# A cross-attention stage in four groups under way at once, ahead of a gated local-attention loop on one core

## The chip, the core and the metric

The kernel runs on one core of a Trainium2 chip. The metric is the device time of one execution in microseconds. A profiled execution gives a span (first to last instruction) and a time of its own that is a little longer.

## What is computed

The input is x, 16 items of 128 tokens by 128 features in float32, and a context of the same shape.

```python
x = x + tanh(g_xattn) * xattn(layernorm(x), ctx)      # 1: the cross stage
x = x + tanh(g_ffn) * ffn(layernorm(x))               # 2: six layers

def xattn(query, value):
    q = query @ Wq.T + bq + qk_b
    v = value @ Wv.T + bv
    attn = softmax(q @ v.T / sqrt(128 / 16))
    return attn @ v
```

Each of the six layers of `ffn` is a local attention of 16 heads of 64 with rotary embeddings, normalised q and k, a window of 32 tokens and the one before it, and then a layer norm with a gated GELU product; both with a residual. Their weights are read once per layer.

## The kernel before

The program is written by hand for each engine: five instruction streams that meet on semaphores. It has two parts.

**The pair loop** takes 48 pairs of items (6 layers by 8 pairs), software-pipelined over three iterations by a `step` function per engine, with a fixed order on each. It is not changed. It reads x, normalised and transposed, from a tile R (features on the partitions), in a half that is shifted by one token. At its head TensorE waits until all of R is there (`h_ready`, 8 pairs) and until the eight weight blocks of layer 0 are split into an upper part (ScalarE, `upper_part`, L498) and a lower part (GpSimd, `lower_part`, L387). SyncE loads these blocks into a ring of four slots: block k + 4 is issued once the lower part of block k is done, and a load is issued only once the one before it has landed (L319 to L323). ScalarE's first instruction of the loop is L550 (xsh, the upper part of the first pair of R), then GpSimd makes xsl (L396), and TensorE's first products are L1049.

**The cross stage** comes ahead of it. It works on groups of 4 items, one 128x512 tile for each step. The loop `Fori(0, 2)` on each engine takes two groups (j = 0, 1) in a turn, each phase for both of them before the next phase:

- VectorE: statistics of the rows (L745, 4 per group), their aggregation (L751), after ScalarE's inverse deviation (L505, L507) four normalisations (L757) into xh4.
- TensorE: four turns (L993); for vT a 512-column product of Wv with the context (L997), for v four products (L999), for q a 512-column product (L1002); four products for the scores (L1006); four turns of p (L1012); four products for the output (L1017); four turns of the normalised result (L1022). A float32 product is two passes, a turn is one.
- ScalarE: copies out of PSUM (L515, L528), q and vT with their biases (L518, L519), exp with row sums (L523), the copies into R (L538).
- VectorE: v plus its bias (L774), row maxima and their negative (L778, L780), one over the sums times the gate (L784, L786), the gated residual into X1 (L791), then statistics and normalisation again, of X1.
- GpSimd: tables TC and TS (L468, L471), for each turn a copy of the context to a tile that TensorE reads (L480), and four lower parts. ScalarE's four upper parts of a turn stand behind its copies of p.

The second turn begins when the first has turned its results (`c_hT`, since xh4, X_ and the other tiles exist twice only). SyncE issues x and the context in halves (8 items each) and three arrays of constants; all engines wait for the first two halves and all constants together (`in_ready`, 5 transfers), and for the other halves at the second turn.

## Time and profile before

| | |
|---|---|
| median of 3 runs | 1537.67 us (1535.64 to 1537.88) |
| profiled execution, its own time | 1537.92 us |
| its span | 1536.0 us |
| mean granted TensorE clock | 0.971 |
| busy: TensorE (PE), its weight loads (PEld) | 94%, 76% |
| busy: VectorE (DVE), ScalarE (ACT), GpSimd (POOL) | 85%, 83%, 77% |

Times in rows are microseconds from the start of the span unless marked ns. A row of a timeline has the start, the time until the last of the merged instructions ended, the engine, the line, the operation, the tile written and those read, how many instructions are merged (x8), and in brackets the idle time before it and what ended that. SPq is SyncE's queue of DMA issues. Two instructions that follow one another on an engine overlap a little, so eight of them take less than eight times the duration of one. PEclk is the granted TensorE clock as a share of 2.4 GHz. A tile that shares its memory with another shows under the other's name: xh4, xhT4, qT4 and vT4 are "u", v4 is "sq", the x input is "OT", the context "v".

### The profile page before, as it was taken

The numbers are of one execution on the slowest core, as the hardware profiler recorded it, in microseconds if no ns is written. First come the engines' busy times: TensorE is split into PE (matmuls) and PEld (weight loads), VectorE is DVE, ScalarE is ACT, GpSimd is POOL, SyncE is SP. The second block draws the span as 40 slices with busy tenths as digits, with TensorE's granted clock in tenths as the row PEclk, the third lists the DMA queues.
The fourth block names the chain that finished last, engine by engine and source line by source line (L and its number), as shares of the span: only waits on it lengthen the run. The fifth ranks groups of instructions, "written<-read, shape, count | busy, mean of one in ns | idle before, by whom it ended". The sixth has DMA issues, their size and how long they took to land.

```text
span 1536.0 us, 84937 instructions
## 1 busy us (share of the span) xinstructions
PE 1439.3 (94%) x33248; PEld 1160.3 (76%) x33248; DVE 1301.4 (85%) x2401; ACT 1272.5 (83%) x2523; POOL 1184.8 (77%) x1166
## 2 busy tenths in 40 slices
PE   4579999999999999999999999999999999999986
PEld 3457777778778788777777777777877777887875
DVE  4577899899899899899989989988989978998962
ACT  3458889889889889889888988988988977888873
POOL 2287888888888888888888888888888866887850
PEclk9679999999999999999999999999999989999998
DMA  5111110111010011011012011012001001100101
GB/s 144 50 35 30 39 43 27 37 57 49 27 54 27 27 58 59 27 47 33 27 37 79 27 37 43 27 32 84 27 20 41 20 23 57 41 20 20 41 22 29
DMA packets 41464, 62.44 MB, mean 41 GB/s; under 512 B 3662, under 2 KB 30412, under 8 KB 41420
## 3 DMA queue, kind: packets, MB, share of 16 engines
q1 hardware_dynamic: 41420, 61.84, 13.6%
q8 instruction: 29, 0.48, 0.1%
q14 instruction: 15, 0.12, 0.0%
HBM read 18.84 MB, written 1.05 MB: 13 GB/s over the span
## 4 chain that ended last, share of the span: by engine, by line
PE 90%; issue 4%; DVE 1%; POOL 1%; ACT 0%; POOLq 0%; DVEq 0%; ACTq 0%
PE bank L1129 13%; PE bank L1049 13%; PE bank L1062 12%; PE bank L1141 11%; PE bank L1102 9%; PE bank L1050 9%; PE bank L1051 9%; PE bank L1176 4%; PE bank L1165 2%; PE bank L1167 2%; PE bank L1166 2%; PE bank L1149 2%; PE bank L1155 1%; DVE t L830 0%; POOL u L416 0%
## 5 line engine op out<-in xcount | busy, mean ns | idle before, releaser
L402 POOL TENSOR_TENSOR u<-u,t 128x512 f32<-128x512 f32 x384 | 490.6, 1283 | 30.3 <-DVE t L830 15.8
L416 POOL TENSOR_TENSOR u<-u,rn 128x512 f32<-128x512 f32 x384 | 390.7, 1044 | 41.9 <-ACT rn L568 41.9
L1049 PE MATMUL bank<-Wl,xsh 128*128 (+1 forms) x576 | 287.1, 498 | 22.6 <-issue 17.1
L422 POOL TENSOR_TENSOR P<-P,rs 128x512 f32<-128x512 f32 x192 | 196.4, 1043 | 132.1 <-DVE rs L858 132.1
L821 DVE TENSOR_TENSOR u<-bank,TC 128x512 f32<-128x512 f32 x384 | 259.8, 677 | 43.4 <-ACT sq L557 42.5
L557 ACT ACTIVATE sq<-bank 128x512 f32<-128x512 f32 x384 | 228.0, 606 | 71.7 <-PE bank L1051 70.1
L830 DVE TENSOR_TENSOR t<-bank,TS 128x512 f32<-128x512 f32 x384 | 257.8, 682 | 1.4
L814 DVE TENSOR_REDUCE ss<-sq 128x8 f32<-128x512 f32 x384 | 253.1, 669 | 6.5 <-issue 6.5
L1050 PE MATMUL bank<-Wh,xsl 128*128 (+1 forms) x576 | 231.2, 401 | 0.0
L1051 PE MATMUL bank<-Wh,xsh 128*128 (+1 forms) x576 | 230.5, 400 | 0.0
L582 ACT COPY qkT<-bank 128x512 f32<-128x512 f32 x384 | 209.9, 600 | 13.0 <-PE bank L1062 10.7
L1129 PEld LDWEIGHTS bank<-PT,vs 64*64 64x64 f32 x6144 | 175.3, 137 | 33.9 <-issue 33.7
L1129 PE MATMUL bank<-PT,vs 64*64 64x32 f32 x6144 | 192.7, 223 | 7.3 <-DVE t L830 2.0
L1129 PE MATMUL bank<-PT,v 64*64 64x32 f32 x6144 | 192.9, 222 | 4.0 <-issue 4.0
L838 DVE TENSOR_REDUCE nm<-bank 128x8 f32<-128x512 f32 x192 | 127.7, 686 | 78.9 <-PE bank L1102 78.9
L1141 PE MATMUL bank<-OT,WoS 128*128 128x256 f32 x768 | 181.6, 391 | 2.8 <-ACT OT L608 2.8
L1129 PEld LDWEIGHTS bank<-PT,v 64*64 64x64 f32 x6144 | 176.6, 138 | 3.6 <-issue 3.6
L1141 PEld LDWEIGHTS bank<-OT,WoS 128*128 128x128 f32 x768 | 145.5, 194 | 34.1 <-issue 15.4
L1049 PEld LDWEIGHTS bank<-Wl,xsh 128*128 128x128 f32 x576 | 110.1, 191 | 58.2 <-issue 35.5
L1062 PEld LDWEIGHTS bank<-shape_constants,u 64*128 64x128 f32 x3072 | 109.1, 141 | 59.3 <-issue 59.3
L1102 PE MATMUL bank<-qkT 64*32 64x64 f32 (+1 forms) x12288 | 150.1, 219 | 3.3 <-issue 3.3
L1102 PEld LDWEIGHTS bank<-qkT 64*32 64x32 f32 x12288 | 129.7, 106 | 29.7 <-issue 22.1
(98 smaller groups left out, 2764.3 us busy)
## 6 DMA issues: line engine op xcount, KB each, us to landing
vs<-v SPq DMA_DIRECT2D x96, 384.0 KB, 3.3
Wraw<-in_L_ffn_Wqkv_dram SPq DMA_DIRECT2D x72, 117.5 KB, 2.1
WoS<-in_L_ffn_Wo_dram SPq DMA_DIRECT2D x6, 512.0 KB, 3.8
W1h<-Wh SPq DMA_DIRECT2D x6, 341.0 KB, 2.5
W1l<-Wl SPq DMA_DIRECT2D x6, 341.0 KB, 2.9
Wraw<-in_L_ffn_W_dram SPq DMA_DIRECT2D x12, 116.0 KB, 2.2
OT<-in_x_dram SPq DMA_DIRECT2D x2, 512.0 KB, 5.7
v<-in_ctx_dram SPq DMA_DIRECT2D x2, 512.0 KB, 7.0
```

The costliest lines, as they stand in the source:

```text
L402: nc.gpsimd.tensor_tensor(u[:, r, c], u[:, r, c], t2[:, r, c % 2], ALU.add).then_inc(add_done[c], 1)
L416: nc.gpsimd.tensor_tensor(by_head(u[:, r, c]), by_head(u[:, r, c]), spread(rn[:, r, HC * c:HC * c + HC], HC, DH), ALU.mult).then_inc(qk_re ...
L814: nc.vector.tensor_reduce(ss[:, r, HC * c:HC * c + HC], by_head(square_out(c, r)), AX, ALU.add).then_inc(ss_done[c], 1)
L821: nc.vector.tensor_tensor(by_head(u[:, r, c]), by_head(bank_of("chunk", c, r)[:]), TC[:, layer(it - lag), c % 2].broadcast_to([128, HC, DH ...
L830: nc.vector.tensor_tensor(halves(t2[:, r, c % 2]), halves(bank_of("chunk", c, r)[:])[:, :, ::-1, :], TS[:, layer(it - lag), c % 2].broadca ...
L1049: nc.tensor.matmul(out, x[0], Wl[:, w], start=True, stop=False)
L1050: nc.tensor.matmul(out, x[1], Wh[:, w], start=False, stop=False)
L1051: nc.tensor.matmul(out, x[0], Wh[:, w], start=False, stop=True).then_inc(done, 1)
L1062: i = nc.tensor.transpose(bank_of(kind, k + g, r)[:, at:at + 64], src[p, 128 * t:128 * t + 128], ident[p, 64 * g:64 * g + 64])
L1102: i = nc.tensor.matmul(bank_of("scores", e, r)[64 * w2 + 32 * a:64 * w2 + 32 * a + 32, at + (32 if w == 0 else 0):at + 64], qkT[f, s, 0, t ...
L1129: i = nc.tensor.matmul(bank_of("values", h, r)[64 * e:64 * e + 64, 64 * t + 32 * w2:64 * t + 32 * w2 + 32], (vs, v)[w2][p, r, head:head + ...
L1141: i = nc.tensor.matmul(bank_of("Wo")[:, 0:2 * S], WoS[:, k], OT[:, k].rearrange("p r s -> p (r s)"), start=(k == 0), stop=(k == INNER // 1 ...
```

## The change

- The groups are four tiles each instead of two: all tiles of the stage, their small statistics tiles, and two PSUM banks per group (CROSS_A, CROSS_B) in place of two banks for each of four uses.
- The two-turn loops are gone. Each engine has one function for each step and group, and a written order of the calls, in which groups are at different steps.
- The inputs come in more parts, each with its semaphore: x and the context for group 0, for group 1, and for groups 2 and 3 together; the gate's two numbers alone; the other constants apart. An engine waits only for what a step reads.
- TensorE reads the context in place; GpSimd's copies of it are gone. GpSimd clears vs, which VectorE did.
- vT goes through ScalarE alone (its own semaphore), before v is computed, as both use bank B. p overwrites xh4, its turned form overwrites xhT4.
- ScalarE's upper parts 0 to 3 stand behind the copy of p of group 1, 4 to 7 one by one between later steps, each with a wait for its own block. GpSimd's lower parts come in one row behind the tables.

The diff, cut to its core (helpers that only wrap an instruction of before with its wait are left out):

```diff
-        cT = [t2[:, 0, g] for g in range(2)]
-        xh4, xhT4, qT4, vT4, p4, pT4, v4 = ([slots[g][j] for g in range(2)] for j in range(7))
+        xh4, xhT4 = ([u[:, k, g] for g in range(GROUPS)] for k in range(2))
+        qT4 = [t2[:, g // 2, g % 2] for g in range(GROUPS)]
+        vT4 = [qkT[:, g // 2, g % 2].rearrange("p t n -> p (t n)") for g in range(GROUPS)]
+        v4 = [PT[:, g // 2, g % 2] for g in range(GROUPS)]
+        p4, pT4 = xh4, xhT4
...
-        X_, V_, VT_, Q_ = K[0:2], K[2:4], K[4:6], K[6:8]
+        CROSS_A, CROSS_B = K[0:4], K[4:8]
...
+        def arrived(eng, sems_of_parts, g):
+            eng.wait_ge(sems_of_parts[min(g, 2)], 16)
...
         @block.sync
...
-            sp.dma_start(H[:, 0:PAIR], x[0:PAIR].rearrange("b s d -> s b d")).then_inc(in_ready, 16)
-            sp.dma_start(ctxS[:, 0:PAIR], ctxT[0:PAIR].rearrange("b d s -> d b s")).then_inc(in_ready, 16)
-            sp.dma_start(sc[:], shape_consts).then_inc(in_ready, 16)
-            sp.dma_start(fc[:], by_feature).then_inc(in_ready, 16)
-            sp.dma_start(ev[:], every_token.partition_broadcast(128)).then_inc(in_ready, 16)
-            sp.sem_inc(rest_ready, START)
-            sp.dma_start(H[:, PAIR:NB], x[PAIR:NB].rearrange("b s d -> s b d")).then_inc(rest_ready, 16)
-            sp.dma_start(ctxS[:, PAIR:NB], ctxT[PAIR:NB].rearrange("b d s -> d b s")).then_inc(rest_ready, 16)
+            items(x, H, "b s d -> s b d", 0, GB, x_in[0])
+            sp.dma_start(ev[:, 128:130], every_token[128:130].partition_broadcast(128)).then_inc(gate_in, 16)
+            sp.dma_start(fc[:], by_feature).then_inc(features_in, 16)
+            items(ctxT, ctxS, "b d s -> d b s", 0, GB, ctx_in[0])
+            sp.dma_start(sc[:], shape_consts).then_inc(shapes_in, 16)
+            items(x, H, "b s d -> s b d", GB, 2 * GB, x_in[1])
+            items(ctxT, ctxS, "b d s -> d b s", GB, 2 * GB, ctx_in[1])
+            sp.dma_start(ev[:, 0:128], every_token[0:128].partition_broadcast(128)).then_inc(rows_in, 16)
+            sp.dma_start(ev[:, 130:], every_token[130:].partition_broadcast(128)).then_inc(rows_in, 16)
+            items(x, H, "b s d -> s b d", 2 * GB, NB, x_in[2])
+            items(ctxT, ctxS, "b d s -> d b s", 2 * GB, NB, ctx_in[2])
...
         @block.gpsimd
...
-            pool.wait_ge(in_ready, 16 * N_INPUTS)
+            nc.gpsimd.memset(vs[0:32], 0.0).then_inc(consts_done, 1)
+            pool.wait_ge(rows_in, 32)
+            pool.wait_ge(shapes_in, 16)
...
-            with pool.Fori(0, NB // PAIR) as pair:
-                pool.wait_ge(rest_ready, pair * 32 + START)
-                for j in range(2):
-                    g = pair * 2 + j
-                    pool.wait_ge(c_v, g - 1 + START)
-                    pool.sem_inc(wait_met, 1)
-                    nc.gpsimd.tensor_copy(cT[j], ctxS[:, ds(g * GB, GB)].rearrange("p b d -> p (b d)")).then_inc(c_ctx, 1)
-                for i in range(4):
-                    lower_part(pair * 4 + i, pair * 4 + i)
+            for k in range(NB // 2):
+                lower_part(k, k)
...
         @block.scalar
...
+            def first_upper(k):
+                act.wait_ge(raw_loaded, 32 * (k + 1))
+                upper_part(k, k)
...
+            cross_rstd(0, 0)
+            cross_vT_out(0)
+            cross_rstd(1, 0)
+            cross_vT_out(1)
+            cross_rstd(2, 0)
+            cross_vT_out(2)
+            cross_x_out(0)
+            cross_rstd(3, 0)
+            cross_vT_out(3)
+            cross_q_out(0)
+            cross_x_out(1)
+            cross_q_out(1)
+            cross_exp(0)
+            cross_x_out(2)
+            cross_x_out(3)
+            cross_p_out(0)
+            cross_exp(1)
+            cross_q_out(2)
+            cross_q_out(3)
+            cross_p_out(1)
+            first_upper(0)
+            first_upper(1)
+            first_upper(2)
+            first_upper(3)
+            cross_exp(2)
+            cross_rstd(0, 1)
+            cross_exp(3)
+            cross_p_out(2)
+            cross_rstd(1, 1)
+            cross_p_out(3)
+            first_upper(4)
+            cross_h_out(0)
+            first_upper(5)
+            cross_h_out(1)
+            first_upper(6)
+            first_upper(7)
+            cross_rstd(2, 1)
+            cross_rstd(3, 1)
+            cross_h_out(2)
+            cross_h_out(3)
...
         @block.vector
...
+            cross_stats(0, 0)
+            cross_stats(1, 0)
+            cross_stats(2, 0)
+            cross_norm(0, 0)
+            cross_stats(3, 0)
+            cross_norm(1, 0)
+            cross_norm(2, 0)
+            cross_norm(3, 0)
+            cross_values(0)
+            cross_maxima(0)
+            cross_values(1)
+            cross_values(2)
+            cross_values(3)
+            cross_maxima(1)
+            cross_gates(0)
+            cross_attend(0)
+            cross_gates(1)
+            cross_stats(0, 1)
+            cross_maxima(2)
+            cross_attend(1)
+            cross_maxima(3)
+            cross_stats(1, 1)
+            cross_norm(0, 1)
+            cross_gates(2)
+            cross_gates(3)
+            cross_norm(1, 1)
+            cross_attend(2)
+            cross_attend(3)
+            cross_stats(2, 1)
+            cross_stats(3, 1)
+            cross_norm(2, 1)
+            cross_norm(3, 1)
...
         @block.tensor
...
+            def cross_v(g):
+                pe.wait_ge(c_vTs, g + 1)
+                for dst, src in zip(tiles(CROSS_B[g]), rows(ctxS, g)):
+                    i = nc.tensor.matmul(dst, src, wvT[:], start=True, stop=True)
+                i.then_inc(c_v, 1)
...
+            pe.wait_ge(features_in, 16)
+            pe.wait_ge(shapes_in, 16)
+            cross_vT(0)
+            cross_vT(1)
+            cross_v(0)
+            cross_vT(2)
+            cross_v(1)
+            cross_x(0)
+            cross_vT(3)
+            cross_q(0)
+            cross_x(1)
+            cross_v(2)
+            cross_scores(0)
+            cross_q(1)
+            cross_v(3)
+            cross_x(2)
+            cross_scores(1)
+            cross_x(3)
+            cross_p(0)
+            cross_q(2)
+            cross_o(0)
+            cross_q(3)
+            cross_p(1)
+            cross_scores(2)
+            cross_scores(3)
+            cross_o(1)
+            cross_p(2)
+            cross_p(3)
+            cross_h(0)
+            cross_o(2)
+            cross_o(3)
+            cross_h(1)
+            cross_h(2)
+            cross_h(3)
```

## Rows read from the trace of the kernel before

**Rows 1.** The page, part 4: the chain that ended last, shares by engine.
```profile
PE 90%; issue 4%; DVE 1%; POOL 1%; ACT 0%; POOLq 0%; DVEq 0%; ACTq 0%
```

**Rows 2.** Stretches: length, busy us (instructions) of each engine, granted clock, DMA share, GB/s.
```profile
9.80:40.11 30.31, 16.73 (x80) 12.70 (x80) 17.02 (x73) 14.77 (x41) 10.11 (x14) 0.85 0.39 107
40.11:68.15 28.04, 16.43 (x80) 12.08 (x80) 13.44 (x60) 13.81 (x40) 4.59 (x4) 0.74 0.11 29
68.15:119.40 51.25, 37.64 (x557) 28.16 (x559) 33.70 (x58) 26.11 (x53) 38.02 (x37) 0.70 0.15 45
119.40:1530.00 1410.60, 1367.37 (x32521) 1106.36 (x32517) 1233.53 (x2204) 1216.03 (x2388) 1131.58 (x1107) 0.99 0.13 38
```

**Rows 3.** Waits in the first 75 us: total, times, longest.
```profile
PE bank L993 <- DVE u L757: 18.3, 2, 14.3
```

**Rows 4.** Second halves' issues; landing times of x (first, last), then of the context.
```profile
3.82 0.38 SPq L308 DMA_DIRECT2D OT<-in_x_dram  x1
4.24 0.80 SPq L309 DMA_DIRECT2D v<-in_ctx_dram  x1
...
DMA to landing us min/median/max: 3.8/5.7/7.7
...
DMA to landing us min/median/max: 5.1/7.0/9.0
```

**Rows 5.** Timeline of VectorE in the cross stage.
```profile
9.26 0.16 DVE L738 TENSOR_TENSOR bqs<-feature_columns 128x1 f32<-128x1 f32 x1 [2.94 <-DMA every_token_rows<-in_every_token_dram]
...
12.38 2.94 DVE L757 TENSOR_SCALAR u<-OT,mv,rstd 128x128 f32 x8 [0.28 <-ACT rstd L507]
18.73 0.69 DVE L774 TENSOR_TENSOR sq<-bank,every_token_rows 128x512 f32<-128x512 f32 x1 [3.42 <-PE bank L999]
...
23.09 0.69 DVE L778 TENSOR_REDUCE mx<-bank 128x4 f32<-128x512 f32 x1 [1.06 <-PE bank L1006]
23.82 0.17 DVE L780 TENSOR_SCALAR nm<-mx 128x4 f32<-128x4 f32 x1
...
25.63 0.18 DVE L784 RECIPROCAL rc<-sum 128x4 f32<-128x4 f32 x1
25.84 0.23 DVE L786 TENSOR_SCALAR rg<-rc,tg 128x4 f32<-128x4 f32 x1
...
32.73 1.64 DVE L745 BATCH_NORM_STATS2 st<-X 128x6 f32 x8
34.30 0.62 DVE L751 BATCH_NORM_AGGREGATE mv<-st 128x2 f32<-128x6 f32 x8
35.26 2.14 DVE L757 TENSOR_SCALAR u<-X,mv,rstd 128x128 f32 x8 [0.34 <-ACT rstd L507]
...
58.44 2.16 DVE L791 SCALAR_TENSOR_TENSOR X<-bank,rg,OT 128x128 f32 x8 [1.41 <-PE bank L1017]
```

**Rows 6.** Timeline of TensorE's products and of one group's exp.
```profile
17.64 1.05 PE L999 MATMUL bank<-feature_columns,t 128*128 128x128 f32 x8
18.53 1.02 PE L1002 MATMUL bank<-u,feature_columns 128*128 128x512 f32 x2
...
24.02 0.37 ACT L523 ACTIVATE PT<-bank,nm 128x128 f32<-128x128 f32 x1 [0.56 <-DVE nm L780]
...
25.31 0.21 ACT L523 ACTIVATION_READ_ACCUMULATOR PT<-bank,nm 128x1 f32 x1
...
27.85 3.42 PE L1017 MATMUL bank<-sq,qkT 128*128 128x128 f32 x16
```

**Rows 7.** Timeline of ScalarE at the end of the cross stage.
```profile
65.76 2.37 ACT L538 COPY R<-bank 64x512 f32 x4 [2.10 <-PE bank L1022]
68.15 0.41 ACT L550 CAST xsh<-R 128x256 fp32r<-128x256 f32 x1
```

**Rows 8.** Timeline of the lower parts and of the block loads behind the first.
```profile
29.44 4.59 POOL L387 TENSOR_TENSOR Wl<-Wraw,Wh 128x470 f32 x4 [15.22 <-ACT Wh L498]
...
30.65 5.61 SPq L323 DMA_DIRECT2D Wraw<-in_L_ffn_Wqkv_dram  x5
```

More of the change, by code:

```diff
@@ L26 @@
 GB = 4
+GROUPS = NB // GB
 CROSS_HEADS = 16
@@ L290, in part_block, with rows, whole, by_item @@
             return W[:, ds((k // (NB // 2)) % 2 * W_SPLIT_SIZE + block * BLOCK, BLOCK)]
-        PAIR = 2 * GB
+        def rows(t, g):
+            return [t[:, GB * g + k] for k in range(GB)]
+        def whole(t, g):
+            return t[:, GB * g:GB * g + GB].rearrange("p b d -> p (b d)")
+        def by_item(ap):
+            return ap.rearrange("p (b d) -> p b d", b=GB)
+        def arrived(eng, sems_of_parts, g):
+            eng.wait_ge(sems_of_parts[min(g, 2)], 16)
         def tiles(t):
@@ L488, in _ @@
         def _(act):
[L489 removed]
+            for s in ACT_SEMS:
                 act.sem_inc(s, START)
[L491 removed]
+            act.wait_ge(gate_in, 16)
             nc.scalar.activation(tg[:], gate2[:], ACT.Tanh).then_inc(tanh_done, 1)
@@ new lines, in cross_p_out, with cross_h_out @@
+            def cross_p_out(g):
+                act.wait_ge(c_pT, g + 1)
+                nc.scalar.copy(pT4[g], CROSS_A[g][:]).then_inc(c_pTs, 1)
+            def cross_h_out(g):
+                act.wait_ge(c_hT, g + 1)
+                for k in range(2):
+                    p = slice(64 * k, 64 * k + 64)
+                    i = nc.scalar.copy(R[p, GB * g:GB * g + GB, k:k + S],
+                                       CROSS_A[g][p].rearrange("p (b s) -> p b s", b=GB))
+                i.then_inc(h_ready, GB // 2)
@@ L730, in _ @@
         def _(dve):
-            for s in DVE_SEMS + [c_st, c_mv, c_xh, c_vs, c_mx, c_nm, c_rc, c_rg, c_x1, c_hn]:
+            for s in DVE_SEMS:
                 dve.sem_inc(s, START)
@@ new lines, in cross_stats @@
+            def cross_stats(g, s):
+                if s == 0:
+                    arrived(dve, x_in, g)
+                else:
+                    dve.wait_ge(c_x1, g + 1)
+                for t, row in enumerate(rows((H, X1)[s], g)):
+                    i = nc.vector.bn_stats(st4[:, g, t], row)
+                i.then_inc(c_st[s], 1)
+                dve.wait_ge(c_st[s], g + 1)
+                for t in range(GB):
+                    i = nc.vector.bn_aggr(mv4[:, g, t], st4[:, g, t])
+                i.then_inc(c_mv[s], 1)
@@ new lines, in cross_attend @@
+            def cross_attend(g):
+                dve.wait_ge(c_rg, g + 1)
+                dve.wait_ge(c_o, g + 1)
+                for t, (dst, row) in enumerate(zip(rows(X1, g), rows(H, g))):
+                    i = nc.vector.scalar_tensor_tensor(out=dst, in0=tiles(CROSS_B[g])[t], scalar=rg4[:, g, t:t + 1],
+                                                       in1=row, op0=ALU.mult, op1=ALU.add)
+                i.then_inc(c_x1, 1)
+            cross_stats(0, 0)
+            cross_stats(1, 0)
@@ new lines, in cross_turn, with cross_x, cross_vT @@
+            def cross_turn(g, bank, src, done):
+                for dst, part in zip(tiles(bank), tiles(src)):
+                    i = nc.tensor.transpose(dst, part, ident[:])
+                i.then_inc(done, 1)
+            def cross_x(g):
+                pe.wait_ge(c_xh[0], g + 1)
+                cross_turn(g, CROSS_A[g], xh4[g], c_xT)
+            def cross_vT(g):
+                arrived(pe, ctx_in, g)
+                nc.tensor.matmul(CROSS_B[g][:], wvT[:], whole(ctxS, g), start=True, stop=True).then_inc(c_vT, 1)
```

236 lines of the change are left out of this document (86 added, 150 removed).

## The prediction

> **What bounds the kernel now.** I read the page first. The chain that ended last lies 90% on TensorE, over a span of 1536.0 us [rows 1]: the pair loop is TensorE's. The stretches then show that this is true only of the loop. From 119.40 us on TensorE is busy 1367.37 of 1410.60 us at a granted clock of 0.99. In the two turns of the cross stage, 30.31 and 28.04 us long, no engine is busy for much more than half: TensorE 16.73 and 16.43, VectorE 17.02 and 13.44, ScalarE 14.77 and 13.81 [rows 2]. That is a stage bound by latency: one phase at a time, two groups in it, everybody else waiting. The waits say the same: TensorE alone stood 18.3 us for the first normalised rows [rows 3]. The loop begins when ScalarE makes xsh, at 68.15 us, directly behind the last copies into R [rows 7]. So the question is one number: at what time L can that instruction start in the changed kernel? The loop's code is untouched, so the time changes by L minus 68.15, plus what a different start does to the loop's first iterations.
>
> **When the stage can start.** Before, all engines wait for five inputs; VectorE is released by the last of them at 9.26 [rows 5]. Afterwards group 0 needs 256 KB alone. The first half of x, 512 KB, landed 3.8 us behind its issue [rows 4], so I put the first quarter at 3.9 us; group 1, with 1.3 MB issued up to it, I put near 7.6, between the landings of the first and the last half. But VectorE's new order is stats 0, stats 1, stats 2, and only then norm 0, and group 2 comes with the last half of x. It was issued at 3.82 and landed 7.7 us later, at 11.5 [rows 4]. The bytes ahead of it are the same, split in more transfers, so I take 11.5 again; it stalls all of VectorE until then. The last ctx landed at 4.24 + 9.0 = 13.2 [rows 4], and TensorE's third product waits for it. The gain of the early start is thus small: norm 0 falls at 12.7 where it was at 12.38 [rows 5]. What the parts give is products of groups 0 and 1 done before.
>
> **VectorE's sum from there.** It is the busiest engine, so I add it up. One group costs: statistics half of 1.64 + 0.62, with the new wait of the aggregation for its own statistics 1.18 (the waits on its own result at 23.82 and 25.84 cost 0.03 to 0.04); four norms half of 2.14, 1.07; values 0.69; maximum and its negative 0.69 + 0.17; gates 0.18 + 0.23; four residuals half of 2.16, 1.08 [rows 5]. Left from 11.5: six statistics 7.1, eight norms 8.6, four values 2.8, four maxima 3.4, four gates 1.6, four residuals 4.3: 27.8 us. Unhindered it would end at 11.6 + 27.8 = 39.4.
>
> **Where it still waits.** TensorE at full clock takes 0.86 for a 512-column product (18.53 minus 17.64, the pitch, is 0.89 for eight 128-column ones) and 0.43 for four turns (four passes in place of eight) [rows 6]. From the last ctx: vT2 0.86, v1 0.89, x0 0.43, vT3 0.86, q0 0.86, x1 0.43, v2 0.89, scores 0 1.1, with 0.3 for a copy: 19.9. VectorE is free at 11.6 + 2 stats + 4 norms + values = 18.9: 1.0 of wait. Residual 0 wants exp (24.02 to the end of the row at 25.31, 1.5 [rows 6]), a turn 0.9, a copy 0.6, a product 1.05, two copies of x ahead on ScalarE 1.1 and handovers 0.3 behind the maximum's end at 20.8: 26.2, against 24.1 at which VectorE has done its other work: 2.1. Smaller ones 0.4. Together 3.5.
> **TensorE's clock.** Eight passes take 1.05 at the upper level; sixteen took 3.42 at 27.85, 0.21 each and so the lower level (1.2 GHz) [rows 6]. The stage now begins with products at 7 us; until some 13.7 I count them low, which costs 0.9 on the way to x0. Bounds: nothing, if it rises by 11; 2.0 if only at 17. TensorE has nothing to do between its last output product and norm 2, some 5 us in my layout, and behind that I count the lower level again.
> **VectorE beside GpSimd.** Eight norms took 2.94 while GpSimd built tables and copied, 2.14 alone [rows 5]. Norm 0 meets the tables; norms of the second half now meet the lower parts (eight of them, 4.59 per four [rows 8]), a meeting that the trace of before doesn't have: between 0 and 0.4 each for three of them by the nearest row, and up to a lower part's 1.15 by its length. I take 0.8 in all, nearer to the row; bounds 0.4 and 3.8.
> The Trainium skill (SBUF — State Buffer, Who interferes with whom) is against this change here: GpSimd and such a VectorE operation share a port pair, and the second "fully blocks" until the first is over. By it each of three norms could lose a whole GpSimd instruction; the sum would be 2.6 us longer, the time 1519.4 rather than 1516.8. The row of 2.94 is milder, though above the norm alone.
>
> **The tail and the sum.** Behind the last norm: handovers 0.1, a turn at the lower clock 1.15, two copies into R 1.19 (four took 2.37 [rows 7]): 2.4. L = 39.4 + 3.5 + 0.9 + 0.8 + 2.4 = 47.0.
> Is another engine later? In the two turns before ScalarE worked 28.6 us in all and TensorE 33.2, partly at the lower clock [rows 2]; spread over L, both fit. GpSimd's four ctx copies go (nothing gained, they were covered), and the memset of vs moves to it, before 4 us, where it is idle. The weights: upper part 0 is now behind p_out 1, near 29; then lower part 1.15, four block loads at 2.2 (five issues in 5.61 [rows 8]), upper and lower part 1.8: the eighth lower part at 42 or so, 5 us ahead of L. If that cover went, every us beyond would be paid. SP's loads 8 to 11 and the copies to W1h follow, done by 49; up wants them only two iterations later.
> Gain: 68.15 − 47.0 = 21.1. I count the loop's start as before: its first 51 us ran at a mean clock of 0.70 [rows 2], and how that pattern falls now is unknown, 3 us either way. Profiled execution: 1537.92 − 21.1 = 1516.8; its own time is 0.25 above the median of the runs shown, which I leave.
>
> **Rivals.**
> *The clock stays low in the stage (9%).* The first turn had 0.85 and the second 0.74 with TensorE busy at about 55% [rows 2]. All of it low, TensorE's products and turns left from 13.2 (20 us at the upper level: 0.86, 0.89 and 0.43 each, for four groups less the three done) take 40 and 8 more of gaps and tail: L near 62, a time of 1532. Low for half the stage, L near 53, 1523. Against it: TensorE's work is now denser. For it: pauses of 1.9, 1.5 and 5 us in my layout. The skill's rule (TensorE: Matmul & The Clock Gate, Part 1: The HAM clock gate) that the throttled state is the default and activity releases it would give this rival where my gaps count as idleness; the trace agrees that it fell behind thin stretches.
> *The stage gains, the loop gives back (7%).* VectorE, ScalarE and GpSimd start the loop in other relations, with more of it at the lower clock: 5 to 8 us back, 1522 to 1525.
> *Better than the sum (10%).* Clock high from 11 on and into the loop, no collision with GpSimd: L 44.5 and 2 us less in the first iterations, 1512.
> *Weights become the bound (2%).* If a block load took 4 us rather than 2.2, the eighth lower part comes at 49 and L is overtaken by 2 us: 1519.
> *Slower than before (2%).* One mechanism: the loop's low clock. In the loop a us at the lower level costs half a us where TensorE bounds. The first 51.25 us had some 31 at that level, as (1 − 0.70) / 0.5 of them [rows 2]. It decides once over 42 us more are low (twice 21.1); with 60 more the time is 1516.8 + 30 = 1547. The kernel's behaviour from 119.40 on (0.99) speaks against it.
> That the change doesn't do what it says (1%): an engine's order could make the groups run one behind another; at 28 us for two groups as now nothing is gained but the 5 us of the input wait, 1533. The written orders speak against it.
>
> **Numbers.** The forecast has 69%, 1516.8. The range 1511 to 1524 takes L from 44.5 to 51 and the loop's 3 us; the lowest of the better case and the half-low clock fit in, the rest is left out. 0.2% is 3.1 us, about what a measurement of this kernel can tell from no change. Only the last mechanism ends slower, 0.02; a hundredth lies within, and the rest, 0.97, is faster by more.
>
> **What would show it.** The first statistics at about 4 us, norm 0 near 12.7, VectorE nearly without a break from 20 on, TensorE's last turns behind norms 2 and 3, xsh at 47, the eighth lower part before 43, and the loop from its second layer on moved by a constant. Norm 0 much before 12, xsh behind a lower part, or a stretch of clock 0.5 in the middle of the stage would show steps wrong. A loop that is longer than 1467.85 us from xsh to the end would point to the second rival.

## The result and the profile after

The changed kernel takes 1519.82 us (median of 4, 1516.7 to 1520.05), the kernel before in the same comparison 1536.66 (1535.21 to 1537.88): a ratio of 0.9878, 95% interval 0.9859 to 0.9897. Forecast were 1516.8 us and a range of 1511 to 1524. The profiled execution took 1519.64 us, 18.3 less than that of before (1537.92).

The page of the changed kernel: its span, the granted clock in 40 slices and the chain's shares (as in [rows 1]):

```profile
span 1517.7 us, 84772 instructions
...
PEclk9789999999999999999999999999999999999998
...
PE 91%; issue 4%; DVE 1%; POOL 1%; ACT 0%; POOLq 0%; DVEq 0%; ACTq 0%
```

Its stretches, columns as in [rows 2]; the first is the cross stage, the second the loop, the others are inside and behind the stage's last third:

```profile
0.00:48.93 48.93, 29.26 (x160) 21.73 (x160) 31.11 (x136) 29.99 (x83) 15.18 (x19) 0.91 0.48 132
48.93:1517.60 1468.67, 1403.76 (x33088) 1132.19 (x33088) 1269.39 (x2264) 1242.40 (x2440) 1170.26 (x1144) 0.98 0.13 38
36.40:39.70 3.30, 3.30 (x18) 3.30 (x17) 2.19 (x9) 2.21 (x5) 2.24 (x2) 0.50 0.26 73
39.90:43.10 3.20, 0.41 (x4) 0.17 (x2) 3.05 (x17) 2.63 (x6) 0.90 (x2) 1.00 0.34 91
43.30:53.30 10.00, 5.07 (x15) 3.82 (x16) 3.64 (x12) 4.30 (x9) 2.15 (x3) 0.50 0.47 150
```

The stage now ends at 48.93 us where it ended at 68.15. Its work is what it was: VectorE is busy for 31.11 us of the 48.93, where the two turns before had 17.02 and 13.44 of 58.35 [rows 2]. The low stretches are now short ones: 36.4 to 39.7 lies on the output products of the last two groups, 39.9 to 43.1 is TensorE's pause at 1.00, and 43.3 to 53.3 takes in the last turns and the loop's first products. The 0.91 leaves the head out: the view has 1.00 there, but TensorE's first four passes, from 8.25 on, took 3.93 us, 0.98 each, where a pass of the same product took 0.43 at the upper level (two of them between 17.32 and 18.18). In the page the clock is 9 from the fourth of the 40 slices to the last but one, and the chain is TensorE's to 91%. The loop takes 1517.7 − 48.93 = 1468.8 us against 1467.85: 0.9 us more, which is less than it scatters between executions (below).

ScalarE's timeline at the end of the stage, to be held against [rows 7]:

```profile
46.54 2.37 ACT L547 COPY R<-bank 64x512 f32<-64x512 f32 x4 [2.50 <-PE bank L1069]
48.93 0.41 ACT L606 CAST xsh<-R 128x256 fp32r<-128x256 f32 x1
```

VectorE's timeline in the stage, to be held against [rows 5] (from 13.54 on its waits, in brackets, come to 3.8 us in all):

```profile
13.54 0.87 DVE L801 BATCH_NORM_STATS2 st<-OT 128x6 f32<-128x128 f32 x4 [3.39 <-DMA OT<-in_x_dram]
...
14.74 1.53 DVE L812 TENSOR_SCALAR u<-OT,mv,rstd 128x128 f32<-128x128 f32 x4
...
17.38 3.13 DVE L812 TENSOR_SCALAR u<-OT,mv,rstd 128x128 f32<-128x128 f32 x12
...
21.54 0.69 DVE L824 TENSOR_REDUCE mx<-bank 128x4 f32<-128x512 f32 x1 [0.43 <-PE bank L1094]
...
24.63 0.69 DVE L824 TENSOR_REDUCE mx<-bank 128x4 f32<-128x512 f32 x1 [0.39 <-PE bank L1094]
...
27.46 1.13 DVE L839 SCALAR_TENSOR_TENSOR X<-bank,rg,OT 128x128 f32<-128x128 f32 x4 [1.60 <-PE bank L1105]
...
38.28 1.13 DVE L839 SCALAR_TENSOR_TENSOR X<-bank,rg,OT 128x128 f32<-128x128 f32 x4 [0.82 <-PE bank L1105]
39.98 1.12 DVE L839 SCALAR_TENSOR_TENSOR X<-bank,rg,OT 128x128 f32<-128x128 f32 x4 [0.58 <-PE bank L1105]
...
43.39 2.97 DVE L812 TENSOR_SCALAR u<-X,mv,rstd 128x128 f32<-128x128 f32 x8
```

SyncE's issues of the last half of x and of the context (against [rows 4]):

```profile
5.41 0.43 SPq L317 DMA_DIRECT2D OT<-in_x_dram  x1
5.89 2.68 SPq L317 DMA_DIRECT2D v<-in_ctx_dram  x1
```

The landing times of the parts of x, over all of them:

```profile
DMA to landing us min/median/max: 2.8/5.6/8.1
```

Those of the context:

```profile
DMA to landing us min/median/max: 4.2/6.3/9.1
```

The last half of x lands at 5.41 + 8.1 = 13.5 and the context at 5.89 + 9.1 = 15.0. Before it was 11.5 and 13.2.

TensorE's timeline at the end of the stage: sixteen passes of the output products of groups 2 and 3 in 3.58 us, then a pause until the last two groups are normalised:

```profile
36.30 3.58 PE L1105 MATMUL bank<-PT,u 128*128 128x128 f32 x16
...
45.38 2.14 PE L1069 MATMUL bank<-shape_constants,u 128*128 128x128 f32 x8 [5.07 <-DVE u L812]
```

GpSimd's timeline at the same time: two lower parts, the second of them beside the last eight norms, and then nothing until xsl:

```profile
42.31 2.42 POOL L407 TENSOR_TENSOR Wl<-Wraw,Wh 128x470 fp32r<-128x470 f32 x2 [2.30 <-ACT Wh L512]
49.50 0.72 POOL L416 TENSOR_TENSOR xsl<-R,xsh 128x256 fp32r<-128x256 f32 x1 [4.77 <-issue]
```

The second of these lower parts by itself, and the eight norms one by one (the shortest, the median and the longest in ns, then the starts of the first and the last):

```profile
43.44 1.29 POOL L407 TENSOR_TENSOR Wl<-Wraw,Wh 128x470 fp32r<-128x470 f32 x1
...
L812 DVE TENSOR_SCALAR u<-X,mv,rstd x8: 316/334/1202, 43.4 to 46.0; 128x128 f32<-128x128 f32 x8
```

Seven of the eight norms took about 0.33 us. One, from 43.62 to 44.82, took 1.20: it ended 0.1 us behind the lower part, at 44.73. The earlier lower part ended as the norms began.

### The profile page after: what moved, and what is told of

It is laid out like the page before. It is cut to its first block, busy times and chain, and to the rows that moved or that the text cites. A ratio compares the mean times of both kernels' runs of the same rounds, so it can differ in the third digit from the quotient of the medians.

```text
span 1517.7 us, 84772 instructions
## 1 busy us (share of the span) xinstructions
PE 1433.0 (94%) x33248; PEld 1153.9 (76%) x33248; DVE 1300.5 (86%) x2400; ACT 1272.4 (84%) x2523; POOL 1185.4 (78%) x1163
## 4 chain that ended last, share of the span: by engine, by line
PE 91%; issue 4%; DVE 1%; POOL 1%; ACT 0%; POOLq 0%; DVEq 0%; ACTq 0%
PE bank L1252 13%; PE bank L1172 13%; PE bank L1185 12%; PE bank L1264 12%; PE bank L1225 9%; PE bank L1173 9%; PE bank L1174 9%; PE bank L1299 4%; PE bank L1288 3%; PE bank L1290 2%; PE bank L1289 2%; PE bank L1272 2%; PE bank L1278 1%; POOL u L422 0%; POOL u L436 0%
## 5 line engine op out<-in xcount | busy, mean ns | idle before, releaser
L1172 PE MATMUL bank<-Wl,xsh 128*128 (+1 forms) x576 | 286.4, 497 | 23.7 <-issue 17.4
L900 DVE TENSOR_TENSOR u<-bank,TC 128x512 f32<-128x512 f32 x384 | 259.8, 677 | 41.8 <-ACT sq L613 40.8
L1264 PEld LDWEIGHTS bank<-OT,WoS 128*128 128x128 f32 x768 | 144.8, 194 | 34.0 <-issue 15.5
L1225 PE MATMUL bank<-qkT 64*32 64x64 f32 (+1 forms) x12288 | 150.4, 219 | 5.2 <-issue 5.2
```

What stands on the lines that cost most here:

```text
L900: nc.vector.tensor_tensor(by_head(u[:, r, c]), by_head(bank_of("chunk", c, r)[:]), TC[:, layer(it - lag), c % 2].broadcast_to([128, HC, DH ...
L1172: nc.tensor.matmul(out, x[0], Wl[:, w], start=True, stop=False)
L1225: i = nc.tensor.matmul(bank_of("scores", e, r)[64 * w2 + 32 * a:64 * w2 + 32 * a + 32, at + (32 if w == 0 else 0):at + 64], qkT[f, s, 0, t ...
L1264: i = nc.tensor.matmul(bank_of("Wo")[:, 0:2 * S], WoS[:, k], OT[:, k].rearrange("p r s -> p (r s)"), start=(k == 0), stop=(k == INNER // 1 ...
```

## The experiments

All of them are measured by the start of xsh in their profiled execution, since the loop behind it, unedited, scatters by more than most edits are worth. Where rounds were timed, the median stands too. xsh scatters as well: two executions of one kernel (e8 and f1) are 1.8 us apart, and the statistics of group 2, which start when the last half of x lands, began at 13.54 and 12.61 in two executions of the changed kernel. The profiles of e1 to e4, of e5 to e8, and of the f runs with the repetition also come from three chips. A difference of xsh under 2 us between two of them shows nothing by itself; the durations and waits in the rows do.

**e1: the overlap undone.** All tiles, banks, semaphores, transfers stay; only the three written orders change.

```diff
             cross_stats(0, 0)
             cross_stats(1, 0)
+            cross_norm(0, 0)
+            cross_norm(1, 0)
...
+            cross_norm(0, 1)
+            cross_norm(1, 1)
             cross_stats(2, 0)
-            cross_norm(0, 0)
...
```

> Same tiles, banks, inputs in parts and no copies of the context, but the written orders take groups 0 and 1 through all steps and then groups 2 and 3. Theory (the gain is the overlap of four groups): xsh, the loop's first instruction on ScalarE, goes from 48.9 back to about 61 us (58 to 64), span near 1530. Rival (the gain comes from the early inputs, the missing copies and the missing turn boundary): xsh at 50 to 53, span near 1520.

xsh came at 64.62, span 1531.0. Its VectorE timeline, norms 0 and 1, statistics and norms of the second pair, and the last norms:

```profile
9.94 3.13 DVE L812 TENSOR_SCALAR u<-OT,mv,rstd 128x128 f32<-128x128 f32 x8
...
35.13 0.86 DVE L801 BATCH_NORM_STATS2 st<-OT 128x6 f32<-128x128 f32 x4
...
59.94 2.11 DVE L812 TENSOR_SCALAR u<-X,mv,rstd 128x128 f32<-128x128 f32 x8
```

And xsh in its ScalarE timeline:

```profile
64.62 0.40 ACT L606 CAST xsh<-R 128x256 fp32r<-128x256 f32 x1
```

The first pair of groups takes 25.2 us from its norms to the next pair's statistics, and the second 23.7 from its norms (38.36) to the end of its last ones. Of the 19.2 us that the change gained in the stage, 15.7 (64.62 − 48.93) are the overlap of the four groups, and 3.5 the rest. Some 2 us of the 15.7 are TensorE's lower level in e1's second pair: its eight turns took 2.14 and its four passes for vT 2.70, where they take 1.04 and 1.72 (four times 0.43) at the upper level. Of the 3.5, the first norms' earlier start is 2.4 (9.94 against 12.38); what the rest is made of wasn't told apart. The expected 61 was too low by 3.6, outside its 58 to 64; the rival's 50 to 53 is out.

**e2: the seven input transfers of before, with their gating.** The eleven issues that they replace are left out.

```diff
+            sp.dma_start(H[:, 0:2 * GB], x[0:2 * GB].rearrange("b s d -> s b d")).then_inc(x_in[0], 16)
+            sp.dma_start(ctxS[:, 0:2 * GB], ctxT[0:2 * GB].rearrange("b d s -> d b s")).then_inc(x_in[0], 16)
+            sp.dma_start(sc[:], shape_consts).then_inc(x_in[0], 16)
+            sp.dma_start(fc[:], by_feature).then_inc(x_in[0], 16)
+            sp.dma_start(ev[:], every_token.partition_broadcast(128)).then_inc(x_in[0], 16)
+            sp.dma_start(H[:, 2 * GB:NB], x[2 * GB:NB].rearrange("b s d -> s b d")).then_inc(x_in[2], 16)
+            sp.dma_start(ctxS[:, 2 * GB:NB], ctxT[2 * GB:NB].rearrange("b d s -> d b s")).then_inc(ctx_in[2], 16)
...
+                eng.wait_ge(x_in[0], 80)
```

> The changed kernel with the seven input transfers of before and their gating (all engines wait for the first five, groups 2 and 3 for the last two). Theory (VectorE's chain starts at the landing of the last half of x, which the parts made later, 13.5 where it was 11.5): xsh at 47.5 us (46.5 to 49), no loss. Rival (the early start of groups 0 and 1 is worth what it looks like, 3 to 4 us): xsh at 52 or later.

xsh at 48.54, span 1518.0. The statistics of group 2 and norm 0 in its VectorE timeline:

```profile
11.96 0.84 DVE L799 BATCH_NORM_STATS2 st<-OT 128x6 f32<-128x128 f32 x4
...
13.13 1.09 DVE L810 TENSOR_SCALAR u<-OT,mv,rstd 128x128 f32<-128x128 f32 x4
```

They begin 1.6 us earlier than with the parts (11.96 and 13.54), though nothing starts before 9.5. The parts gave the four-group stage nothing that these runs can see: they let groups 0 and 1 run ahead and made the last half late. Of the 1.6, 1.34 are there at the first maximum (20.20 against 21.54), and 0.4 at xsh. Most of the loss lies at the output products of group 2, for which VectorE waited 1.48 us rather than 0.82: this execution had a lower clock from 33.1 to 39.9, twice as long as the changed kernel's 36.3 to 39.8. Another 0.2 is the last eight norms, 3.16 us.

**e3: the rotary rows last.**

```diff
-            sp.dma_start(ev[:, 130:], every_token[130:].partition_broadcast(128)).then_inc(rows_in, 16)
             items(x, H, "b s d -> s b d", 2 * GB, NB, x_in[2])
             items(ctxT, ctxS, "b d s -> d b s", 2 * GB, NB, ctx_in[2])
+            sp.dma_start(ev[:, 130:], every_token[130:].partition_broadcast(128)).then_inc(tabs_in, 16)
```

> The 384 KB broadcast of the rotary rows is issued behind all x and context, so that the last half of x lands some 1.3 to 1.8 us earlier. Theory (VectorE's chain from that landing): norm 0 at 13.2 rather than 14.7; xsh 47.6, or 48.3 if GpSimd's tables, now at 15 to 19 us, slow norms 1 to 3 as they slowed norm 0. Rival (TensorE and ScalarE's chain is late anyway): xsh at 48.9.

xsh at 47.25, span 1516.1. Its VectorE timeline, statistics of group 2, norm 0 and norms 1 to 3:

```profile
11.44 0.87 DVE L801 BATCH_NORM_STATS2 st<-OT 128x6 f32<-128x128 f32 x4 [1.64 <-DMA OT<-in_x_dram]
...
12.64 1.08 DVE L812 TENSOR_SCALAR u<-OT,mv,rstd 128x128 f32<-128x128 f32 x4
...
14.83 4.75 DVE L812 TENSOR_SCALAR u<-OT,mv,rstd 128x128 f32<-128x128 f32 x12
```

The last half of x is there 2.1 us earlier and norm 0 stands at 12.64. GpSimd's tables now run beside norms 1 to 3: twelve normalisations in 4.75 us, where the changed kernel took 3.13. The end came 1.7 us earlier all the same, earlier than both of the theory's times. Against the changed kernel's second execution (below) it is 1.2 at the landing and 1.5 at the end. The last context came earlier too: TensorE, which had waited 1.77 us for it, went on at 13.10 without a wait. So the end of the stage follows the last inputs, even with the dearer norms; e3 doesn't tell x from the context.

Later in the same execution the four norms of group 1 met a lower part, and it shows on one of them alone:

```profile
35.47 1.18 POOL L407 TENSOR_TENSOR Wl<-Wraw,Wh 128x470 fp32r<-128x470 f32 x1 [2.47 <-ACT Wh L512]
...
L812 DVE TENSOR_SCALAR u<-X,mv,rstd x4: 340/341/1280, 34.7 to 35.5; 128x128 f32<-128x128 f32 x4
```

**e4: the last lower parts behind the norms.**

```diff
             for k in range(NB // 2):
+                if k == NB // 2 - 2:
+                    pool.wait_ge(c_xh[1], GROUPS)
                 lower_part(k, k)
```

> GpSimd's last two lower parts wait until the last normalisations are done. Theory (the eight norms at 43.4 took 2.97 us where eight alone take 2.14, because a lower part runs beside them): 2.14 again, xsh at 48.1 us, the lower parts at 45.6 to 48. Rival (something else slows them): 2.97 and xsh at 48.9. If the lower parts become the last thing the loop waits for, TensorE's first product comes over 1.5 us behind xsh.

The last eight norms in its VectorE timeline:

```profile
44.51 2.14 DVE L814 TENSOR_SCALAR u<-X,mv,rstd 128x128 f32<-128x128 f32 x8
```

2.14 us for eight, as alone, none over 0.345, so the lower part beside them was the cause of the 2.97. But xsh came at 49.22, not 48.1. Its x had landed 0.4 later (statistics of group 2 at 13.92), and the lower clock lay at 34.7 to 41.5, all over the output products of groups 2 and 3; the statistics behind them began 0.7 us later against those of group 2's x than before (28.17 and 27.48). The gain and the loss were of one size.

**e5: norm 0 and norm 1 ahead of the statistics of group 2.**

```diff
             cross_stats(0, 0)
+            cross_norm(0, 0)
             cross_stats(1, 0)
+            cross_norm(1, 0)
             cross_stats(2, 0)
-            cross_norm(0, 0)
             cross_stats(3, 0)
-            cross_norm(1, 0)
```

> Only VectorE's order is changed: norm 0 and norm 1 stand directly behind their statistics, before those of group 2, so that they don't wait for the last half of x. Theory (norm 0's wait is covered, since TensorE's turns of group 0 stand in its own order behind the product that waits for the last context, 15.0 us): norm 0 at about 7.5 us and norm 1 at 10.5, but the first maximum still at 21.5 and xsh at 48.9 within 0.5. Rival (VectorE's sum from the landing of x is the path, as the prediction's sum has it): two norms less in it, xsh at 46.8.

xsh at 51.09, later than theory and rival had it. Norm 0, the statistics of group 2 and the first maximum in its VectorE timeline:

```profile
7.10 1.12 DVE L812 TENSOR_SCALAR u<-OT,mv,rstd 128x128 f32<-128x128 f32 x4 [0.69 <-ACT rstd L518]
...
13.38 0.87 DVE L801 BATCH_NORM_STATS2 st<-OT 128x6 f32<-128x128 f32 x4 [0.44 <-DMA OT<-in_x_dram]
...
23.03 0.69 DVE L824 TENSOR_REDUCE mx<-bank 128x4 f32<-128x512 f32 x1 [1.26 <-PE bank L1094]
```

Norm 0 was ready 7.6 us earlier and the first maximum stood 1.5 us later. The granted clock was 0.50 from 14.9 to 18.3, where the changed kernel's first execution had the upper level. Was that the edit's doing? The repetition answers it.

**The changed kernel once more, unedited.**

> The changed kernel once more, unedited, for the scatter of one execution against another. Theory (where TensorE's lower level falls differs between executions; in the first execution it stood at 36.3 to 39.8, in e5 and e7, whose edits come later, also at 15 to 19): xsh between 48.5 and 50.5, the loop between 1464 and 1470, both moved by where the lower level falls. Rival (the level's place is a property of the program): xsh 48.9 and a loop of 1468.8 again, both within 0.3.

The median was 1518.79 (1516.78 to 1522.16; ratio 0.9905, 0.9875 to 0.9935). Its profile has xsh at 48.72, the loop at 1466.2, and a low stretch of its own from 14.0 to 17.4. The statistics of group 2 and the first maximum in its VectorE timeline:

```profile
12.61 0.87 DVE L801 BATCH_NORM_STATS2 st<-OT 128x6 f32<-128x128 f32 x4 [3.28 <-DMA OT<-in_x_dram]
...
22.28 0.69 DVE L824 TENSOR_REDUCE mx<-bank 128x4 f32<-128x512 f32 x1 [1.26 <-PE bank L1094]
```

The low stretch, columns as in [rows 2]:

```profile
14.00:17.40 3.40, 3.14 (x9) 2.11 (x10) 3.37 (x17) 1.12 (x3) 0.54 (x2) 0.50 0.30 77
```

So such a stretch comes without the edit too; it belongs to the execution. From the statistics of group 2 to the first maximum it is 22.28 − 12.61 = 9.67 us here and 23.03 − 13.38 = 9.65 in e5. With like clocks, the place of norms 0 and 1 is worth nothing, as e5's theory had it: TensorE's turns of group 0 stand behind the product with the last context. Both these executions had VectorE wait 1.26 us for TensorE ahead of the maximum. At the upper level VectorE waited there too, 0.43 us, so TensorE was the later one in all three. In the first execution, with the clock high, it was 21.54 − 13.54 = 8.00. The low stretch there costs 1.7 us (9.67 − 8.00), of which 0.16 is a context that came later behind x (1.65 us rather than 1.49). The theory of this run held; its rival's loop of 1468.8 within 0.3 is out.

**e7: TensorE kept busy in its pauses.** The extra turns go to a free bank and are read by nobody.

```diff
+            def keep_busy(n):
+                for k in range(n):
+                    nc.tensor.transpose(tiles(CROSS_A[0])[k % 4], ident[:], ident[:])
...
+            pe.wait_ge(c_pTs, 1)
+            keep_busy(12)
             cross_p(2)
+            pe.wait_ge(c_pTs, 1)
+            keep_busy(12)
             cross_p(3)
...
+            pe.wait_ge(h_ready, START + GB // 2)
+            keep_busy(36)
             cross_h(2)
```

> The changed kernel with 12, 12 and 36 extra turns of the identity into a bank that is free then, in TensorE's pauses before p 2, p 3 and h 2; nobody reads them. Theory (the lower clock at 36.3 to 39.8 and from 43.2 on, behind pauses, makes the output products of groups 2 and 3 take 3.6 us rather than 2.0 and the last turns 2.1 rather than 1.3): no lower level before the loop, output products 2.0, xsh at 47.2 to 47.8, and the loop's first 5 us at the upper level too. Rival (the clock is of no weight, VectorE hides it): xsh 48.9; or the extra turns stand in the way: over 49.5.

Its TensorE timeline:

```profile
37.85 1.95 PE L1105 MATMUL bank<-PT,u 128*128 128x128 f32 x16
...
40.50 4.09 PE L1114 MATMUL bank<-shape_constants 128*128 128x128 f32 x36
46.21 0.66 PE L1069 MATMUL bank<-shape_constants,u 128*128 128x128 f32 x4 [1.62 <-DVE u L812]
...
50.73 0.77 PE L1182 MATMUL bank<-Wl,xsh 128*128 128x512 f32 x1 [2.83 <-POOL xsl L416]
```

The output products took 1.95 us rather than 3.58, the last turns ran at the upper level (0.66 for four), and from the first maximum to xsh it was 49.29 − 23.09 = 26.2 us against 27.4 in the changed kernel. xsh itself came at 49.29, because this execution too had the low stretch at 15.5 to 18.9, ahead of all extra turns. The repetition, with no extra turns and no low stretch there, took 48.72 − 22.28 = 26.4 for the same way: the net gain behind the first maximum is about 1 us. The waits for the output products, 0.82 and 0.58 in the changed kernel, are gone in both, which is 1.4; other delays hide a part of it, 0.67 for the deviations in the repetition and, here, 0.93 for a lower part beside the norms of group 1. The loop's first products were low again from 49.6 on. Of the expectation, the products' 2.0 held; xsh at 47.2 to 47.8 and a loop start at the upper level did not.

**e8: tables last and GpSimd out of the way.** e3 and e4 together, and the tables wait for norm 3.

```diff
             pool.wait_ge(tabs_in, 16)
+            pool.wait_ge(c_xh[0], GROUPS)
...
+                if k == NB // 2 - 2:
+                    pool.wait_ge(c_xh[1], GROUPS)
```

> Tables last as in e3, and GpSimd stays off VectorE's normalisations: it makes the tables only behind norm 3, and the last two lower parts behind the last norm. Theory (the two meetings cost 4.75 - 3.1 = 1.6 and 2.97 - 2.14 = 0.8): norms at 1.05 to 1.1 each, xsh 46.0 (45.5 to 46.8), apart from what TensorE's clock does. Rival (the first norms are covered as in e5's theory, only the last ones count): 46.8 to 47.3.

xsh at 45.53, span 1509.7. The norms in its VectorE timeline:

```profile
12.51 1.08 DVE L815 TENSOR_SCALAR u<-OT,mv,rstd 128x128 f32<-128x128 f32 x4
...
14.70 3.13 DVE L815 TENSOR_SCALAR u<-OT,mv,rstd 128x128 f32<-128x128 f32 x12
...
41.02 2.11 DVE L815 TENSOR_SCALAR u<-X,mv,rstd 128x128 f32<-128x128 f32 x8
```

1.08 for four, 3.13 for twelve, 2.11 for eight. It is 3.4 us better than the changed kernel in the stage, and at the edge of the theory's bounds. 2.2 us of it are x, which landed at 11.31 rather than 13.54. That xsh doesn't stand by itself: the same kernel once more (f1) came to 47.37.

**e6 and f2: new orders.** On top of e8 norms 0 to 2 stand directly behind their statistics and TensorE turns group 0 before the products of groups 2 and 3; e6 has ScalarE's upper parts 4 and 5 behind a copy into R, f2 ahead of it.

```diff
             cross_p_out(3)
+            first_upper(4)
             cross_h_out(0)
+            first_upper(5)
             cross_rstd(2, 1)
-            first_upper(4)
-            first_upper(5)
             cross_h_out(1)
```

> e8 with new written orders on VectorE, ScalarE and TensorE: each norm directly behind its statistics, group 0 turned before the products of groups 2 and 3, first upper parts spread over ScalarE's early gaps. Theory (VectorE's sum from 11.5 less the two early norms, 25.7, with 2.5 of waits, 0.5 for the clock and 2.4 of tail, is 42.6 at best and the handovers leave about 44.5): xsh at 44.5 (43.5 to 46), span near 1513. Rival (some other chain, TensorE's or ScalarE's, is as long as VectorE's): xsh 46 or later.

> e6 with ScalarE's upper parts 4 and 5 ahead of the copies into R, so that lower parts 4 and 5 are over before the last norms. Theory (e6 missed 44.5 because its last eight norms took 2.96 beside lower parts 4 and 5): the norms 2.14, xsh 45.0 to 45.4. Rival (ScalarE's two more casts delay the copies and the last deviations): xsh 46 or later.

e6 has xsh at 46.11 and a span of 1505.3; f2 45.91 and 1509.6, a median of 1512.17 (1510.94 to 1518.21, ratio 0.9865, 0.984 to 0.989). The last eight norms in e6's VectorE timeline:

```profile
40.58 2.96 DVE L815 TENSOR_SCALAR u<-X,mv,rstd 128x128 f32<-128x128 f32 x8
```

And in f2's, with the four of group 1 ahead of them:

```profile
35.34 2.09 DVE L815 TENSOR_SCALAR u<-X,mv,rstd 128x128 f32<-128x128 f32 x4
...
41.23 2.11 DVE L815 TENSOR_SCALAR u<-X,mv,rstd 128x128 f32<-128x128 f32 x8
```

f2's theory is right about the last norms, but the end moved by 0.2 us only. The meeting had moved rather than gone: of the four norms of group 1, 1.11 us in e6, one took 1.33 beside a lower part of 1.23. In e6 the new orders got the first maximum 1.3 us earlier than e8's (18.25 and 19.52), but the second came at 23.54 behind a wait of 1.74 for TensorE, where e8 had it at 22.61 with none. The sum of VectorE's work no longer sets the length by itself, and e6's theory, 44.5, missed; its rival, 46 or later, holds. f2's median is f1's within 0.2 us, so the new orders gained nothing that the rounds can see.

**f1 and f3: e8 timed, and e8 with TensorE kept busy up to the loop** (12, 12 and 30 extra turns as in e7, and 18 behind the last group's turns).

> e8 once more, timed in rounds. Theory: xsh 45.5 to 46.5, 3 to 4 us ahead of the changed kernel in the stage, ratio to before near 0.9845 (1512 to 1514). Rival (e8's total was luck with the clock in the loop): xsh the same, the median at 1516 or more.

> e8 with extra turns of the identity in TensorE's pauses: 12 before p 2 and p 3, 30 before h 2, 18 behind h 3, up to the loop's first product. Theory (e7 showed no lower level from 20 us to the loop, and 1.2 us less from the first maximum to xsh, but the level fell in the pause behind h 3): no lower level from about 20 us on into the loop, xsh 44.8 to 45.3, the loop's first 5 us at 2.4 GHz, and 2 to 3 us off the total of f1. Rival (the level falls in the loop anyway, some iterations later): xsh the same, the total within 1 us of f1's.

f1: median 1512.34 (1511.78 to 1513.17), ratio 0.9855 (0.9831 to 0.9879), xsh at 47.37. f3: 1512.27 (1511.5 to 1514.53), 0.9857 (0.9833 to 0.9882), xsh at 47.22. In the same rounds the changed kernel stood at 1518.79 and the kernel before at 1534.94. So the rotary rows last and GpSimd out of the way are worth some 6 us of the total, of which the stage's profiles show 1.4 to 3.4; the extra turns add nothing. f1's theory held in the total (1512 to 1514) and not in xsh (45.5 to 46.5). Its xsh was 1.8 us behind that of e8, the same kernel: x landed 0.8 later, and the lower clock lasted from 32.7 to 39.6 where e8 had it from 32.6 to 36.0. f3 had the loop's first 5 us at the upper level, but the lower one from 43.3 to 46.7, xsh 2 us later than expected, and a total within 1 us of f1's, as its rival had it. f3 shows what comes next when VectorE is early, in ScalarE's timeline:

```profile
41.45 0.58 ACT L515 CAST Wh<-Wraw 128x470 fp32r<-128x470 f32 x1 [2.81 <-DMA Wraw<-in_L_ffn_W_dram]
```

Upper part 7 waited 2.81 us for its block of weights, and the inverse deviations of groups 2 and 3 stand behind it in ScalarE's order, so the last norms waited 2.39 us for them. The repetition of the changed kernel had the same on a smaller scale, in its ScalarE timeline:

```profile
42.33 0.58 ACT L512 CAST Wh<-Wraw 128x470 fp32r<-128x470 f32 x1 [1.10 <-DMA Wraw<-in_L_ffn_W_dram]
```

## Why the prediction was right, and by how much its steps were off

The direction, the mechanism and the range held; the forecast was 3.0 us below the median. Of the 2.8 by which it missed the profiled execution, 1.9 are xsh and 0.9 the loop. By its own steps:

- *When the stage can start*: the step that failed. It took the last half of x at 11.5 and of the context at 13.2, since the bytes ahead were the same. They came at 13.5 and 15.0: SyncE, with more transfers ahead, issued the last x at 5.41, not at 3.82, and it took 8.1 us to land, not 7.7. In the repetition it landed at 12.6, so 0.9 of the 2.0 is scatter of this one execution. xsh was missed by 1.9 us (48.93 against 47.0); the landing alone is 2.0. Of the two inputs it is the context that the first maximum hung on: VectorE waited 0.43 us for TensorE there, and TensorE's row from the last context to the end of scores 0 took 6.5 us (15.03 to 21.51), where the prediction added up 6.7. The other terms cancelled, which is luck: waits and clock 3.8 against 4.4, GpSimd 1.3 against 0.8, the tail 2.6 against 2.4. In the six executions with the changed kernel's orders (both of its own, e2, e3, e4, e7) the statistics of group 2 began between 11.44 and 13.92 and xsh came 35.3 to 36.6 us behind them.
- *Norm 0 is hardly earlier*: right in kind, 14.74 against 12.38 before. It is even later. The first statistics came at 5.78, not at about 4: the sum of two biases ahead of them waits for the feature columns (5.70). Nothing hung on it, as x of group 2 was the stop.
- *VectorE's sum, 27.8, with waits 3.5, clock 0.9, GpSimd 0.8*: 33.0 from the last half of x to the last norm's end; measured 46.36 − 13.54 = 32.8 (the last norm ends at 43.39 + 2.97). The waits were 0.43, 0.39, 1.60, 0.82 and 0.58, 3.8 in all, where waits and clock together were put at 4.4. GpSimd's part was under-sized: norm 0 took 1.53 (0.46 more) and the last eight 2.97 (0.83 more), 1.3.
- *TensorE's clock*: put at 0.9 on the way to x0. The first products did run at the lower level, but cost nothing, as the next one waited 1.77 for the last context; in the repetition the level fell again during that wait and cost 1.5 to 1.7. The sign that the prediction named, a stretch of 0.5 inside the stage, came at 36.3 to 39.8, and the 1.4 of waits for output products hang on it (none in e7 and in the repetition). The prediction had only the pause behind them low.
- *VectorE beside GpSimd*: the price of a meeting was misjudged. "The row of 2.94 is milder" doesn't hold: in the kernel before, the slow ones of those eight norms took 0.55, 0.63 and 0.63 us beside GpSimd instructions of 0.54, 0.61 and 0.61. The Trainium skill (SBUF — State Buffer, Who interferes with whom) says that the second of the two "fully blocks", and the traces agree: one norm of 1.20 us beside a lower part of 1.29 in the changed kernel, one of 1.28 beside 1.18 in e3, the rest of those eight and four at 0.32 to 0.34. e4 and e8 take GpSimd away and the norms go back to 2.14 and 2.11. What was fewer than the rule's three is the meetings: one of norm with lower part, and two short ones of norm 0 with the tables. That its 1519.4 is so near the 1519.64 is luck, the landing's doing.
- *The tail*: 2.4 predicted, 48.93 − 46.36 = 2.57.
- *The weights as cover*: the eighth lower part was over at 44.7, not 42 (the terms given add up to 40.8), and 4 us ahead of xsh. It was late because upper parts 6 and 7 stand behind the copy into R of group 1, which waited for TensorE until 40.35. That sum looked only at the loop's wait. It missed that ScalarE's wait for block 7 stands ahead of the last inverse deviations: 1.10 us of it in the repetition, 2.81 in f3.
- *The loop as before, 3 us either way*: 1468.8 against 1467.85, and in the repetition 1466.2.
- *Rivals*: the low clock in the stage didn't decide (0.87 on the mean from 13.54 to xsh, up from 0.85 and 0.74 before). The groups did overlap, as e1 shows by undoing it. The loop gave nothing back beyond its scatter.

What stays open is the loop. Its length from xsh to the end was 1468.8 and 1466.2 in the changed kernel, 1466.4, 1469.5, 1468.9, 1467.4 and 1465.7 in e1 to e5, 1464.6 in e7, 1463.9, 1464.2, 1463.7 and 1463.2 in f1, e8, f2 and f3, and 1459.2 in e6, with the same instructions throughout. The granted clock's low stretches fall differently in each. Its middle is the same: from the sixth pair's xsh to the 41st's it is 1022.7 and 1022.8 us in the changed kernel's two executions, 1022.7 in e8 and 1022.8 in f1. The differences lie at its two ends. The first five pairs took 153.6, 150.0, 150.4 and 145.2 us, so one kernel (e8 and f1) scatters there by 5 us. Still, the five profiles with GpSimd out of the way have the five shortest loops of all, and f1's five timed executions all lie 3.5 us or more below the changed kernel's eight (1511.78 to 1513.17, 1516.7 to 1522.16). That is hard to put down to chance, but no run shows what makes the loop shorter. Of the 6 us by which f1 beats the changed kernel in rounds, it is the larger part if f1's own profile is the measure (1.4 in the stage), and half if e8's is (3.4).

## What to carry to other kernels

In this stage no engine was busy for more than 59% [rows 2], and more independent items at different steps paid. Its new length could be had in advance by adding up the busiest engine from the landing of the last input that its written order waits for, plus its waits for the others, here above all for TensorE behind the last context. Here that was right within 0.2 us, with luck among the terms; the same kind of sum missed e6 by 1.6, where VectorE waited 1.84 and 1.74 for TensorE ahead of the first two maxima and one of its last norms met a lower part. Splitting inputs so that the first groups can start early is worth little if an engine's order meets the last input soon after (e2), and each further transfer delays that one by its issue, 0.43 to 0.55 us here. Once a stage is packed, check what stands behind every wait on an in-order engine: here a cast that waited for weights held up two small activations on the path.

## What the runs showed of the hardware that I had not expected

- The place of TensorE's low clock differs between executions of one program: of the changed kernel's two profiles one ran at the lower level from 14.0 to 17.4 us and the other at the upper. That moved the first maximum by 1.5 to 1.7 us of 9.7, more than most edits here, so a single profile can't tell an edit of 1 us from chance unless the low stretches are compared first.
- Eight tensor-scalar normalisations of 128x128 on VectorE take 2.10 to 2.14 us alone and 2.75 to 3.16 beside GpSimd's 128x470 subtractions; twelve take 3.13 alone and 4.75 beside its tables. The loss is not spread: a single normalisation stands until the GpSimd instruction beside it is over (1.20 us beside 1.29, 1.28 beside 1.18, 0.33 otherwise). In e3 six in a row of those beside the tables took 0.44 to 0.90 us each, with a GpSimd instruction of 0.53 to 0.87 beside every one. The GpSimd instruction can be the one that is longer: a lower part that began 0.02 us behind the last norm of group 1 took 1.36 us in the changed kernel, where it takes 1.18 alone.
- The loop, whose instructions no edit touched, took between 1459.2 and 1469.5 us in single profiles.
